# Latent attention: values and router logits made with weights as the stationary side over all 512 tokens, copied by ScalarE and turned by transposes

## The chip, the cores and the metric

The kernel runs on one core of one Trainium2 chip. The metric is the time of one launch on the device, in microseconds; less is better. The engines are TensorE (PE, matrix products and transposes into the PSUM banks), VectorE (DVE), ScalarE (ACT), GpSimd (POOL) and SyncE (SP), which issues most transfers.

## What is computed

Two layers over 8 sequences of 512 tokens with 256 features: softmax attention, a quantized feed-forward net, decaying linear attention, and last a step with latent attention and a sparse mixture of 8 experts. The change is in that last step's attention and router. Cut to it, the reference is:

```python
K = (hs @ k_w + k_b)   # 16 heads of 8
V = (hs @ v_w + v_b)   # 256 -> 128 features: 16 heads of 8
attn = softmax(Q[..., :8] @ K.T / sqrt(8), axis=-1)
ao = attn @ V                                   # 512 x 128, padded with zeros
mla_out = ao @ o_w + o_b                        # 512 x 256
probs = softmax(mla_out @ router_w + router_b)  # 512 x 8
topw, topi = top_k(probs, 2)
```

## The kernel before

Five parts run one after the other, each a block with its own program for every engine. The one of the change is `latent_attention` (from L1461). It handles one sequence per round and overlaps two: while the attention of one sequence is computed, the next one is loaded, turned and projected ("ahead"). A loop (`Fori`, in `turns`) runs 7 rounds; the ahead steps of the first sequence stand before it, and the rest of the last sequence behind it.

A round has 64 gaps (0 to 63), one for every unit of scores: 4 groups `a` of 4 heads, 4 blocks `t` of 128 keys, 4 heads `s`. The function `put(gap, engine, step)` places each step by hand, and every engine works through its steps strictly in the order of the gaps. Within a gap the pair S and ST comes first (A and TM ahead of it), and the steps that were put later stand behind. The steps, as "name(gap)" where the gap matters:

- S: scores of a unit, one product of 512 columns into one of 3 banks (`mla_ps_s`); M on VectorE takes their maximum. S of a bank waits for the M that empties it. S at gap 14 is the first unit of the next sequence; it needs the padded keys of that sequence and the M of gap 13.
- ST: the same scores, turned and shifted by the maximum, into one of 2 banks (`mla_ps_t`); X on ScalarE takes the exponential into `mla_pt`. ST waits for the X two units back.
- A: after every fourth unit, 4 products (8 instructions in the trace), probabilities times values (`mla_v`). OT copies the sum out.
- T, XH, XL: the next sequence's input is turned by TensorE and split into a high part (`xth`, ScalarE) and a low part (`xtl`, VectorE), so that three fp32r products give one product of full precision. `sum_of_parts` (L105 to L110) issues those three for each of the two blocks of 128 features; all its products carry line L110.
- Y(1) at gap 4, Y(0) at gap 6: queries and keys of the next sequence, weights stationary, 512 tokens moving: 6 products each for two column ranges. YH and YL split the results. Then SyncE copies them into `stack` (3 transfers for each side) and from there into `pad` (8 transfers, 4 for S and 4 for ST) for each group of heads.
- V at gap 10: the values. For each of 4 token blocks the tokens are the stationary side and the weights (128 columns) the moving one: 24 products of 128x128 into one bank `m`, so that the tokens lie on the partitions, as A needs them. VB on VectorE at gap 12 adds the bias (broadcast to all partitions) and copies to `vn`; VV on GpSimd copies into `mla_v` at gap 36.
- After the last A: BT, RI, AO, CT, CH, CL turn and split the attention's output; MT, MH and ML (gaps 50 to 53) make `mla_out` with the features on the partitions (`mth`, `mtl`).
- RL at gap 54: the router's logits, tokens stationary and the 8 columns of `router_w` moving, for 4 token blocks: 24 products of 128x8. LG on VectorE at gap 55 adds the bias, EX on ScalarE the exponential, and 21 small steps on VectorE up to gap 61 pick two experts. MO(0) and MO(1) at gaps 55 and 57 give `mla_out` with tokens on the partitions; POS at gap 62, PLACES and SC write the rows to the experts' lists.

All steps on TensorE but S, ST and A share two banks (`ps_m`) in turn; `emptied` names for each which engine's step frees its bank.

Of the kernel before, what the change touches and what calls it, by code (L numbers as in the profile page):

```python
# [21 lines left out]
ACT = mybir.ActivationFunctionType  # L22
# [3 lines left out]
P = 128  # L26
# [1434 lines left out]
def latent_attention(nc, const, x_in, sorted_out, counts, pieces_in, w, name):  # L1461
# [8 lines left out]
    with ctx:  # L1470
# [12 lines left out]
        vb, orow, rrow = sb("vb", [P, LAT]), sb("orow", [P, D]), sb("rrow", [P, E_])  # L1483
# [55 lines left out]
        def put(gap, eng, *keys, ahead=False):  # L1539
            if gap >= ROUND:  # L1540
                assert ahead
                gap, ahead = gap - ROUND, False
            gaps.setdefault((gap, eng), []).extend(keys)
            if ahead:
                ahead_keys[eng].update(keys)
# [18 lines left out]
        put(10, "tensor", ("V",), ahead=True); put(12, "vector", ("VB",), ahead=True)  # L1564
# [7 lines left out]
        put(end + 18, "tensor", ("RL",))  # L1572
# [13 lines left out]
        for eng in ("tensor", "vector", "scalar", "gpsimd"):  # L1586
# [6 lines left out]
        emptied = {"T": (dve_s, "XL"), "Y": (dve_s, "YL"), "V": (dve_s, "VB"), "BT": (dve_s, "AO"), "CT": (dve_s, "CL"),  # L1593
                   "POS": (dve_s, "PT"), "MT": (dve_s, "ML"), "MO": (dve_s, "MO"), "RL": (dve_s, "LG"), "TM": (dve_s, "QM")}
# [12 lines left out]
        with nc.Block() as block:  # L1607

            @block.sync
            def _(sp):  # L1610
                weights = [(raw_y[:, :, :], w["base"].rearrange("(k p) n -> p k n", p=P)), (raw_v[:, :, :], w["v_w"].rearrange("(k p) n -> p k n", p=P)),
                           (raw_r[:, :, :], w["router_w"].rearrange("(k p) n -> p k n", p=P)), (raw_o[:, 0, :], w["o_w"][0:P, :])]
                small = [(yb[:, :], w["base_b"]), (one_rows[:, :], w["one_rows"]), (vb[:, :], w["v_b"].partition_broadcast(P)),
# [47 lines left out]
            def _(pe):  # L1661
                own = owner("tensor")
                pe_s.start(pe)
                pe.wait_ge(zeroed, 3)

                def steps(i, run):
                    in_misc = [k for k in run if k in bank]
                    for key in run:
# [19 lines left out]
                        elif kind == "V":  # L1688
                            pe.wait_ge(weights_split, 2)
                            for t in range(TT):  # L1690
                                tok = slice(P * t, P * t + P)
                                last = sum_of_parts(nc, m[:, LAT * t:LAT * t + LAT], lambda k: xth[:, k, tok], lambda k: xtl[:, k, tok], lambda k: wvh[:, k, :], lambda k: wvl[:, k, :], KD)
# [47 lines left out]
                        elif kind == "RL":  # L1740
                            pe.wait_ge(*dve_s.at(j, "ML", KD - 1))
                            for t in range(TT):
                                tok = slice(P * t, P * t + P)
                                last = sum_of_parts(nc, m[:, E_ * t:E_ * t + E_], lambda k: mth[:, k, tok], lambda k: mtl[:, k, tok], lambda k: wrh[:, k, :], lambda k: wrl[:, k, :], KD)
# [13 lines left out]
            def _(dve):  # L1758
# [6 lines left out]
                dve.wait_ge(zeroed, 2)  # L1765
                nc.vector.memset(v[:, :, :, KPH:KPH + 1], 1.0).then_inc(zeroed, 1)
                dve.wait_ge(zeroed, 3)
# [45 lines left out]
                def steps(i, run):  # L1813
                    for key in run:
# [17 lines left out]
                        elif kind == "VB":  # L1832
                            dve.wait_ge(*pe_s.at(j, "V"))
# [644 lines left out]
```

## Time and profile before

| what | us |
|---|---|
| median of 3 runs | 3385.95 (3382.43 to 3387.80) |
| the profiled execution | 3384.29 |
| its span in the trace | 3382.5 |
| TensorE busy, of the span | 2859.8 (85%) |
| VectorE busy | 2033.0 (60%) |
| ScalarE busy | 1337.5 (40%) |
| latent attention in the trace | about 2210 to 3000 |

A row of the timeline has the start in us from the span's start, the length in us, engine, line, operation, output<-input, shape, count, and in brackets the idle time of the engine before it with what ended it. Matmuls overlap: the step from one start to the next is the price in a row of them, and the length is longer. PEld rows are loads of the stationary side.

### The profile page before, as it was taken

What the parts mean: (1) busy time and instruction counts of PE and PEld (TensorE: products, weight loads), DVE (VectorE), ACT (ScalarE), POOL (GpSimd) and SP (SyncE); (2) the same over time, 40 slices, a digit from 0 to 9 for tenths busy, and PEclk for the clock granted to TensorE, in tenths of its full rate; (3) what the DMA queues carried; (4) which work ended last, traced back from release to release, by engine and by line L of the source; (5) the groups of instructions that cost most, each with busy time, mean ns of one, the idle gap of its engine ahead of it and who ended that gap; (6) DMA issues with size and microseconds to landing.
All of it is one profiled execution on the core that took longest, in us unless ns stands there. A gap on an engine that the chain in (4) does not pass through costs nothing. (4 is left out here: it accounts for less than half of the span.)

```text
span 3382.5 us, 61649 instructions
## 1 busy us (share of the span) xinstructions
PE 2859.8 (85%) x16506; PEld 2062.8 (61%) x16507; DVE 2033.0 (60%) x3929; ACT 1337.5 (40%) x2815; POOL 965.4 (29%) x1303
## 2 busy tenths in 40 slices
PE   5998999989999958859999999868888888818992
PEld 4666666666666647747777777635544445417992
DVE  3666656566665568835666666566566566535664
ACT  3555554545545412222222222224444444424443
POOL 4334343343433211123333333210111111121225
PEclk8999999999999979979999999979888888868996
DMA  1101111011111021020000000031222211134225
GB/s 61 38 24 41 39 29 36 30 41 38 29 31 31 30 83 37 31 97 12 11 11 11 12 12 12 7 96 51 62 62 62 61 51 51 30 105 133 72 73 193
DMA packets 124632, 163.92 MB, mean 48 GB/s; under 512 B 19706, under 2 KB 87954, under 8 KB 123794
## 3 DMA queue, kind: packets, MB, share of 16 engines
q1 hardware_dynamic: 113300, 138.40, 13.9%
q0 software_dynamic: 6912, 18.96, 1.5%
q10 hardware_dynamic: 4224, 4.19, 0.4%
q8 instruction: 93, 1.52, 0.2%
q14 instruction: 103, 0.84, 0.1%
HBM read 87.73 MB, written 37.06 MB: 37 GB/s over the span
## 5 line engine op out<-in xcount | busy, mean ns | idle before, releaser
L1115 ACT ACTIVATE soft_probs<-soft_ps_s,soft_mx 128x512 f32<-128x512 f32 x512 | 347.9, 685 | 395.5 <-DVE soft_mx L1034 371.1
L1839 DVE TENSOR_REDUCE mla_mx<-mla_ps_s 128x1 f32<-128x512 f32 x512 | 334.2, 684 | 242.9 <-PE mla_ps_s L1699 225.3
L1034 DVE TENSOR_REDUCE soft_mx<-soft_ps_s 128x1 f32<-128x512 f32 x512 | 329.1, 684 | 236.9 <-PE soft_ps_s L944 224.3
L1942 ACT ACTIVATE mla_pt<-mla_ps_t 128x512 f32<-128x512 f32 x512 | 292.8, 600 | 397.5 <-PE mla_ps_t L1711 361.2
L944 PE MATMUL soft_ps_s<-soft_ks,soft_qs 128*128 128x512 f32 x1024 | 310.8, 423 | 10.3 <-ACT soft_probs L1115 10.3
L953 PE MATMUL soft_ps_p<-ident,soft_probs 128*128 128x128 f32 x2048 | 267.2, 273 | 12.6 <-issue 6.1
L953 PEld LDWEIGHTS soft_ps_p<-ident,soft_probs 128*128 128x128 f32 x2048 | 237.5, 141 | 47.5 <-issue 7.8
L944 PEld LDWEIGHTS soft_ps_s<-soft_ks,soft_qs 128*128 128x128 f32 x1024 | 171.6, 190 | 144.7 <-issue 59.2
L1044 DVE COPY soft_pt<-soft_ps_p 128x512 f32<-128x512 f32 x256 | 175.4, 685 | 137.3 <-PE soft_ps_p L953 134.6
L1699 PE MATMUL mla_ps_s<-mla_stack,mla_pad 128*128 128x512 f32 x512 | 236.0, 468 | 22.4 <-DVE mla_mx L1839 17.4
L962 PE MATMUL soft_ps_a<-soft_pt,soft_v 128*64 128x512 f32 x1024 | 251.9, 614 | 0.0
L1711 PE MATMUL mla_ps_t<-mla_shifted,mla_pad 128*128 128x512 f32 x512 | 226.2, 444 | 27.2 <-ACT mla_pt L1942 24.9
L407 PE MATMUL decay_ps_s<-decay_qs,decay_ks 128*128 128x512 f32 (+3 forms) x1024 | 192.1, 330 | 31.3 <-DVE decay_pt L523 30.5
L523 DVE TENSOR_TENSOR decay_pt<-decay_ps_s,decay_dec 128x512 f32<-128x512 f32 (+3 forms) x512 | 213.4, 480 | 4.7 <-PE decay_ps_s L407 4.7
L649 POOL TENSOR_TENSOR decay_rt<-decay_rt 128x256 f32<-128x256 f32 (+1 forms) x192 | 122.7, 661 | 300.7 <-DVE decay_rt L498 300.7
L407 PEld LDWEIGHTS decay_ps_s<-decay_qs,decay_ks 128*128 128x128 f32 x1024 | 169.2, 195 | 64.3 <-DVE decay_pt L523 44.0
L1699 PEld LDWEIGHTS mla_ps_s<-mla_stack,mla_pad 128*128 128x128 f32 x512 | 104.9, 205 | 165.9 <-DVE mla_mx L1839 74.7
L1122 ACT COPY soft_pt<-soft_ps_p 128x512 f32<-128x512 f32 x256 | 149.8, 585 | 81.5 <-PE soft_ps_p L953 70.5
L498 DVE TENSOR_TENSOR decay_rt<-decay_ps_m,decay_rope 128x1024 f32<-128x1024 f32 (+1 forms) x96 | 100.4, 1046 | 125.3 <-POOL decay_st L654 104.4
L313 ACT CAST decay_st<-decay_rt 128x512 fp32r<-128x512 f32 x64 | 39.6, 619 | 334.9 <-POOL decay_rt L649 197.4
L1711 PEld LDWEIGHTS mla_ps_t<-mla_shifted,mla_pad 128*128 128x128 f32 x512 | 103.0, 202 | 96.2 <-ACT mla_pt L1942 83.1
L1720 PE MATMUL mla_ps_a<-mla_pt,mla_v 128*32 128x512 f32 x1024 | 153.9, 676 | 6.5 <-ACT mla_pt L1942 4.8
(337 smaller groups left out, 6580.7 us busy)
## 6 DMA issues: line engine op xcount, KB each, us to landing
soft_rrep<-inverse SPq DMA_DIRECT2D x128, 128.0 KB, 2.9
mla_pad<-mla_stack SPq DMA_DIRECT2D x256, 64.0 KB, 2.0
moe_xt<-by_expert SPq DMA_DIRECT2D x72, 129.0 KB, 2.1
soft_ks<-soft_ks SPq DMA_DIRECT2D x64, 128.0 KB, 2.3
raw<-in_L_ffn_w SPq DMA_DIRECT2D x16, 512.0 KB, 8.6
mla_stack<-mla_yh SPq DMA_DIRECT2D x128, 64.0 KB, 2.1
soft_xc<-in_L_attn_x SPq DMA_DIRECT2D x8, 512.0 KB, 4.1
soft_xb<-in_L_attn_x SPq DMA_DIRECT2D x8, 512.0 KB, 4.1
```

The source lines that it names most:

```text
L407: last = nc.tensor.matmul(ps_s[:, t, P * t:SEQ], ks[:, n, g, P * t:P * t + P], qs[:, h, P * t:SEQ], start=(n == 0), stop=(n == 1))
L523: op = vv.tensor_tensor(weights_of(h, t), ps_s[:, t, P * t:SEQ], dec[:, h, 0:SEQ - P * t], ALU.mult)
L944: last = nc.tensor.matmul(ps_s[:, s_bank(n), :], qs[:, h, P * t:P * t + P], ks[:, b, g, :], start=(b == 0), stop=(b == 1))
L953: last = nc.tensor.transpose(ps_p[:, c % 2, P * t:P * t + P], probs[:, h % 2, t, P * c:P * c + P], ident[:, :])
L962: last = nc.tensor.matmul(ps_a[HD * s:HD * s + HD, 0, :], v[:, 1, c, HD * g:HD * g + HD], weights_of(2 * p + s, c), start=(c == 0), stop=( ...
L1034: op = vv.tensor_reduce(out=mx[:, h, t:t + 1], in_=ps_s[:, s_bank(4 * h + t), :], axis=AX.X, op=ALU.max, negate=True)
L1044: op = vv.tensor_copy(weights_of(h, c), ps_p[:, c % 2, :])
L1115: op = nc.scalar.activation(probs[:, h % 2, t, :], ps_s[:, s_bank(4 * h + t), :], ACT.Exp, bias=mx[:, h, t:t + 1], scale=1.0, accum_out=rs ...
L1699: last = nc.tensor.matmul(ps_s[:, (4 * t + s + 16 * a) % S_BANKS, :], pad[:, QUADS + a, s, P * t:P * t + P], stack[:, a, :], start=True, s ...
L1711: last = nc.tensor.matmul(ps_t[:, s % 2, :], pad[:, a, s, P * t:P * t + P], shifted[:, a, :], start=True, stop=True)
L1839: op = vv.tensor_reduce(out=mx[:, a, t, s:s + 1], in_=ps_s[:, (16 * a + 4 * t + s) % S_BANKS, :], axis=AX.X, op=ALU.max, negate=True)
L1942: op = nc.scalar.activation(pt[:, t % 2, s, :], ps_t[:, s % 2, :], ACT.Exp, scale=KPH ** -0.5)
```

## The change

V and RL are turned round. The weights become the stationary side and all 512 tokens move: 6 products of 512 columns instead of 24. The result then has the features (or the 8 experts) on the partitions. A copy on ScalarE takes it from PSUM to SBUF (VA to `vt`, with the bias now one value for each partition; RC to `lt`, 8 partitions of 128, of which the rest are set to zero once at the start), and 4 transposes on TensorE bring it back to tokens on the partitions (VT, RT). VB becomes a plain copy; LG adds the bias as before, from every 128th group of 8 columns.

The places move as well: V from gap 10 to 8, VA at 9, VT at 11, VB stays at 12; RL from 54 to 53, RC at 53, RT at 54, LG stays at 55. The two shared banks go on in turn with two more users.

The diff, cut to its core:

```diff
@@ -1480,7 +1480,8 @@
-        vb, orow, rrow = sb("vb", [P, LAT]), sb("orow", [P, D]), sb("rrow", [P, E_])
+        vb, orow, rrow = sb("vb", [P, 1]), sb("orow", [P, D]), sb("rrow", [P, E_])
+        vt, lt = sb("vt", [P, SEQ]), sb("lt", [P, SEQ])
@@ -1561,7 +1562,7 @@
-        put(10, "tensor", ("V",), ahead=True); put(12, "vector", ("VB",), ahead=True)
+        put(8, "tensor", ("V",), ahead=True); put(9, "scalar", ("VA",), ahead=True); put(11, "tensor", ("VT",), ahead=True); put(12, "vector", ("VB",), ahead=True)
@@ -1569,7 +1570,7 @@
-        put(end + 18, "tensor", ("RL",))
+        put(end + 17, "tensor", ("RL",)); put(end + 17, "scalar", ("RC",)); put(end + 18, "tensor", ("RT",))
@@ -1590,8 +1591,8 @@
-        emptied = {"T": (dve_s, "XL"), "Y": (dve_s, "YL"), "V": (dve_s, "VB"), "BT": (dve_s, "AO"), "CT": (dve_s, "CL"),
-                   "POS": (dve_s, "PT"), "MT": (dve_s, "ML"), "MO": (dve_s, "MO"), "RL": (dve_s, "LG"), "TM": (dve_s, "QM")}
+        emptied = {"T": (dve_s, "XL"), "Y": (dve_s, "YL"), "V": (act_s, "VA"), "VT": (dve_s, "VB"), "RT": (dve_s, "LG"), "BT": (dve_s, "AO"), "CT": (dve_s, "CL"),
+                   "POS": (dve_s, "PT"), "MT": (dve_s, "ML"), "MO": (dve_s, "MO"), "RL": (act_s, "RC"), "TM": (dve_s, "QM")}
@@ -1610,7 +1611,7 @@
-                small = [(yb[:, :], w["base_b"]), (one_rows[:, :], w["one_rows"]), (vb[:, :], w["v_b"].partition_broadcast(P)),
+                small = [(yb[:, :], w["base_b"]), (one_rows[:, :], w["one_rows"]), (vb[:, :], w["v_b"]),
@@ -1661,7 +1662,7 @@
-                pe.wait_ge(zeroed, 3)
+                pe.wait_ge(zeroed, 4)
@@ -1687,9 +1688,11 @@
+                            last = sum_of_parts(nc, m, lambda k: wvh[:, k, :], lambda k: wvl[:, k, :], lambda k: xth[:, k, :], lambda k: xtl[:, k, :], KD)
+                        elif kind == "VT":
+                            pe.wait_ge(*act_s.at(j, "VA"))
                             for t in range(TT):
-                                tok = slice(P * t, P * t + P)
-                                last = sum_of_parts(nc, m[:, LAT * t:LAT * t + LAT], lambda k: xth[:, k, tok], lambda k: xtl[:, k, tok], lambda k: wvh[:, k, :], lambda k: wvl[:, k, :], KD)
+                                last = nc.tensor.transpose(m[:, P * t:P * t + P], vt[:, P * t:P * t + P], ident[:, :])
@@ -1739,9 +1742,11 @@
+                            last = sum_of_parts(nc, m[0:E_, :], lambda k: wrh[:, k, :], lambda k: wrl[:, k, :], lambda k: mth[:, k, :], lambda k: mtl[:, k, :], KD)
+                        elif kind == "RT":
+                            pe.wait_ge(*act_s.at(j, "RC"))
                             for t in range(TT):
-                                tok = slice(P * t, P * t + P)
-                                last = sum_of_parts(nc, m[:, E_ * t:E_ * t + E_], lambda k: mth[:, k, tok], lambda k: mtl[:, k, tok], lambda k: wrh[:, k, :], lambda k: wrl[:, k, :], KD)
+                                last = nc.tensor.transpose(m[:, P * t:P * t + P], lt[:, P * t:P * t + P], ident[:, :])
@@ -1762,9 +1767,10 @@
-                dve.wait_ge(zeroed, 2)
+                nc.vector.memset(lt[:, :], 0.0).then_inc(zeroed, 1)
+                dve.wait_ge(zeroed, 3)
                 nc.vector.memset(v[:, :, :, KPH:KPH + 1], 1.0).then_inc(zeroed, 1)
-                dve.wait_ge(zeroed, 3)
+                dve.wait_ge(zeroed, 4)
@@ -1830,9 +1836,9 @@
-                            dve.wait_ge(*pe_s.at(j, "V"))
+                            dve.wait_ge(*pe_s.at(j, "VT"))
                             dve.wait_ge(*pool_s.at(shift(j, -1), "VV"))
-                            op = vv.tensor_tensor(vn[:, :, :], ps_m[:, bank["V",], :].rearrange("p (t n) -> p t n", n=LAT), vb[:, :].unsqueeze(1).broadcast_to([P, TT, LAT]), ALU.add)
+                            op = vv.tensor_copy(vn[:, :, :], ps_m[:, bank["VT",], :].rearrange("p (t n) -> p t n", n=LAT))
@@ -1873,8 +1879,8 @@
-                            dve.wait_ge(*pe_s.at(j, "RL"))
-                            op = vv.tensor_tensor(A3(lg), ps_m[:, bank["RL",], 0:TT * E_].rearrange("p (t e) -> p t e", e=E_), per_expert(rrow), ALU.add)
+                            dve.wait_ge(*pe_s.at(j, "RT"))
+                            op = vv.tensor_tensor(A3(lg), ps_m[:, bank["RT",], :].rearrange("p (t e) -> p t e", e=P)[:, :, 0:E_], per_expert(rrow), ALU.add)
@@ -1923,6 +1929,14 @@
+                        elif kind == "VA":
+                            act.wait_ge(*pe_s.at(j, "V"))
+                            act.wait_ge(*pe_s.at(shift(j, -1), "VT"))
+                            op = nc.scalar.activation(vt[:, :], ps_m[:, bank["V",], :], ACT.Identity, bias=vb[:, 0:1], scale=1.0)
+                        elif kind == "RC":
+                            act.wait_ge(*pe_s.at(j, "RL"))
+                            act.wait_ge(*pe_s.at(shift(j, -1), "RT"))
+                            op = nc.scalar.copy(lt[0:E_, :], ps_m[0:E_, bank["RL",], :])
@@ -2453,6 +2467,7 @@
+    host["L1_ffn_v_b"] = host["L1_ffn_v_b"].reshape(P, 1)
```

What stands on TensorE around V, in the loop. In the names, `mla_ps_s`, `mla_ps_t` and `mla_ps_a` are S, ST and A; L110 is a product of `sum_of_parts`. Before, from ST(8) to A(11), with the 24 products cut to the first three and the last:

```order
2007 L1711 MATMUL mla_ps_t<-mla_shifted,mla_pad 128x512
...
2009 L1699 MATMUL mla_ps_s<-mla_stack,mla_pad 128x512
...
2013 L1699 MATMUL mla_ps_s<-mla_stack,mla_pad 128x512
...
2015 L1711 MATMUL mla_ps_t<-mla_shifted,mla_pad 128x512
2016 L1675 REGISTER_ALU
2017 L110 MATMUL mla_ps_m<-mla_wvh,mla_xth 128x128
2018 L110 MATMUL mla_ps_m<-mla_wvl,mla_xth 128x128
2019 L110 MATMUL mla_ps_m<-mla_wvh,mla_xtl 128x128
...
2040 L110 MATMUL mla_ps_m<-mla_wvh,mla_xtl 128x128
2041 L1714 REGISTER_ALU
2042 L1720 MATMUL mla_ps_a<-mla_pt,mla_v 32x512 x4
```

And of the change, from ST(8) to VT at gap 11:

```order
1990 L1714 MATMUL mla_ps_t<-mla_shifted,mla_pad 128x512
1991 L1676 REGISTER_ALU
1992 L110 MATMUL mla_ps_m<-mla_xth,mla_wvh 128x512
1993 L110 MATMUL mla_ps_m<-mla_xtl,mla_wvh 128x512
...
1997 L110 MATMUL mla_ps_m<-mla_xth,mla_wvl 128x512
1998 L1701 REGISTER_ALU
1999 L1702 MATMUL mla_ps_s<-mla_stack,mla_pad 128x512
...
2007 L1723 MATMUL mla_ps_a<-mla_pt,mla_v 32x512 x4
...
2010 L1714 MATMUL mla_ps_t<-mla_shifted,mla_pad 128x512
...
2013 L1695 MATMUL mla_ps_m<-ident,mla_vt 128x128 x4
```

V now stands two units of scores earlier, ahead of S(9), and the transposes come after the A, S and ST of gap 11.

On TensorE around RL, before, from ST(53) over the 24 products (`mla_wrh`, `mla_wrl` are the router's weights) to A(55):

```order
2255 L1711 MATMUL mla_ps_t<-mla_shifted,mla_pad 128x512
2256 L1698 REGISTER_ALU
2257 L1699 MATMUL mla_ps_s<-mla_stack,mla_pad 128x512
2258 L1710 REGISTER_ALU
2259 L1711 MATMUL mla_ps_t<-mla_shifted,mla_pad 128x512
...
2262 L110 MATMUL mla_ps_m<-mla_wrh,mla_mth 128x8
...
2285 L110 MATMUL mla_ps_m<-mla_wrh,mla_mtl 128x8
...
2288 L1720 MATMUL mla_ps_a<-mla_pt,mla_v 32x512 x4
```

And of the change, from ST(53) to A(55):

```order
2222 L1714 MATMUL mla_ps_t<-mla_shifted,mla_pad 128x512
...
2225 L110 MATMUL mla_ps_m<-mla_mth,mla_wrh 8x512
...
2230 L110 MATMUL mla_ps_m<-mla_mth,mla_wrl 8x512
2231 L1701 REGISTER_ALU
2232 L1702 MATMUL mla_ps_s<-mla_stack,mla_pad 128x512
2233 L1713 REGISTER_ALU
2234 L1714 MATMUL mla_ps_t<-mla_shifted,mla_pad 128x512
2235 L1747 REGISTER_ALU
2236 L1749 MATMUL mla_ps_m<-ident,mla_lt 128x128 x4
...
2239 L1723 MATMUL mla_ps_a<-mla_pt,mla_v 32x512 x4
```

RL now stands ahead of S(54) and ST(54), and the transposes RT stand between them and A(55).

## Rows read from the trace of the kernel before

**Rows 1.** The page: busy time, share of the span and instructions of each engine.

```profile
PE 2859.8 (85%) x16506; PEld 2062.8 (61%) x16507; DVE 2033.0 (60%) x3929; ACT 1337.5 (40%) x2815; POOL 965.4 (29%) x1303
```

**Rows 2.** Timeline of TensorE in the second round, from S(9) to S(14).

```profile
2385.61 0.39 PE L1699 MATMUL mla_ps_s<-mla_stack,mla_pad 128*128 128x512 f32 x1
2388.50 0.80 PE L1711 MATMUL mla_ps_t<-mla_shifted,mla_pad 128*128 128x512 f32 x1 [2.50 <-ACT mla_pt L1942]
...
2390.16 0.31 PE L110 MATMUL mla_ps_m<-mla_wvh,mla_xth 128*128 128x128 f32 x1
...
2395.31 1.94 PE L1720 MATMUL mla_ps_a<-mla_pt,mla_v 128*32 128x512 f32 x8
...
2400.60 0.50 PE L1699 MATMUL mla_ps_s<-mla_stack,mla_pad 128*128 128x512 f32 x1 [1.03 <-DVE mla_mx L1839]
```

**Rows 3.** Stretches: length, busy times, then granted clock, DMA share, GB/s.

```profile
2388.00:2398.00 10.00, 9.50 (x37) 0.50 0.27 67
```

```profile
2290.00:2920.00 630.00, 551.65 (x2635) 313.87 (x2627) 391.82 (x823) 287.06 (x524) 65.97 (x104) 0.88 0.21 56
```

**Rows 4.** Timeline of ScalarE, then VectorE, same round: X(7), X(8) and X(9), YL(0).

```profile
2387.85 0.60 ACT L1942 ACTIVATE mla_pt<-mla_ps_t 128x512 f32<-128x512 f32 x1 [4.36 <-remote]
...
2388.91 1.09 ACT L1942 ACTIVATE mla_pt<-mla_ps_t 128x512 f32<-128x512 f32 x2
...
2389.06 0.75 DVE L1827 SCALAR_TENSOR_TENSOR mla_yl<-mla_ps_m,mla_yb,mla_yh 128x512 fp32r<-128x512 f32 x1
```

**Rows 5.** Timeline of TensorE in the first round: ST(53), RL's first product, A(55), S(55).

```profile
2347.43 0.39 PE L1711 MATMUL mla_ps_t<-mla_shifted,mla_pad 128*128 128x512 f32 x1
...
2349.83 0.27 PE L110 MATMUL mla_ps_m<-mla_wrh,mla_mth 128*128 128x8 f32 x1 [0.89 <-DVE mla_mtl L1831]
...
2354.48 1.94 PE L1720 MATMUL mla_ps_a<-mla_pt,mla_v 128*32 128x512 f32 x8
2356.34 0.80 PE L1699 MATMUL mla_ps_s<-mla_stack,mla_pad 128*128 128x512 f32 x1
```

**Rows 6.** Timeline of VectorE there: ML(1), M(55), LG.

```profile
2349.04 0.74 DVE L1831 SCALAR_TENSOR_TENSOR mla_mtl<-mla_ps_m,mla_ocol,mla_mth 128x512 fp32r<-128x512 f32 x1
...
2357.18 0.69 DVE L1839 TENSOR_REDUCE mla_mx<-mla_ps_s 128x1 f32<-128x512 f32 x1 [6.80 <-PE mla_ps_s L1699]
2357.79 0.18 DVE L1877 TENSOR_TENSOR mla_lg<-mla_ps_m,mla_rrow 128x32 f32<-128x32 f32 x1
```

**Rows 7.** Prices: products of Y, transposes, A and four gaps; a ScalarE copy (min/median/max ns).

```profile
2380.24 0.39 PE L110 MATMUL mla_ps_m<-mla_xth,mla_wyl 128*128 128x512 f32 x1
2380.47 0.40 PE L110 MATMUL mla_ps_m<-mla_xth,mla_wyh 128*128 128x512 f32 x1
...
2401.18 0.61 PE L1704 MATMUL mla_ps_m<-ident,mla_mrow 128*128 128x128 f32 x4
2401.72 1.07 PE L1720 MATMUL mla_ps_a<-mla_pt,mla_v 128*32 128x512 f32 x8
2402.72 0.50 PE L1699 MATMUL mla_ps_s<-mla_stack,mla_pad 128*128 128x512 f32 x1
...
2405.32 1.07 PE L1720 MATMUL mla_ps_a<-mla_pt,mla_v 128*32 128x512 f32 x8
```

```profile
L1947 ACT COPY mla_ot<-mla_ps_a x32: 578/580/590, 2274.1 to 2966.3; 128x512 f32<-128x512 f32 x32
```

**Rows 8.** Pad transfers of the second round; of the first sequence, with S that waits.

```profile
2392.16 5.12 SPq L1637 DMA_DIRECT2D mla_pad<-mla_stack  x8
```

```profile
2238.46 5.07 SPq L1637 DMA_DIRECT2D mla_pad<-mla_stack  x8
```

```profile
2242.41 10.21 PE L1699 MATMUL mla_ps_s<-mla_stack,mla_pad 128*128 128x512 f32 x17 [4.99 <-DMA mla_pad<-mla_stack]
```

**Rows 9.** Timeline of VectorE: memset at the start; LG of the last sequence.

```profile
2224.85 0.91 DVE L1764 MEMSET mla_mrow<- 128x1024 f32 x1 [0.16 <-issue]
...
2978.55 0.19 DVE L1877 TENSOR_TENSOR mla_lg<-mla_ps_m,mla_rrow 128x32 f32<-128x32 f32 x1 [3.00 <-PE mla_ps_m L110]
```

## The prediction

> **What bounds the kernel now.** First the page: TensorE is busy for 85% of the span and no other engine for more than 60% [rows 1]. That is a mean over stages, so the question is what the latent attention's own round looks like: 7 rounds of about 93 us, in each of which one sequence is attended to while the next one is prepared. I name places by the gap (0 to 63) in which the plan puts them. The timeline of TensorE round the step V (gap 10) and round RL (gap 54) is what the change bears on, so I read those two stretches, then the same microseconds on VectorE, ScalarE and SyncE's queue.
>
> At V [rows 2]: after the S of gap 9 TensorE idles 2.50 us for ScalarE; then ST(9), S(10), ST(10), and the 24 products of V, from 2390.16 to the next A at 2395.31, 5.15 us, 0.215 us each. The stretch 2388 to 2398 was granted 0.50 of the clock, which is the lower of the two levels, 1.2 GHz [rows 3]. S(14), the first product with the next sequence's scores, starts at 2400.60. The idle 2.50 us are not V's doing: ScalarE and VectorE both resume at 2387.8, ScalarE after 4.36 us put down to "remote" [rows 4]. Nothing in the code waits there for anything late, and its like stands in each of the 7 rounds. I take it as given.
>
> At RL [rows 5]: ML(1) on VectorE ends at 2349.78 [rows 6]; RL starts at 2349.83 and holds TensorE for 4.65 us until A(55); S(55) follows at 2356.34. Only when its maximum M(55) has run (2357.18) does VectorE come to LG (2357.79), after 6.80 us idle [rows 6]. From there the router's small operations keep VectorE nearly full to gap 62, so that what LG gains the whole tail of the round gains.
>
> So TensorE's in-order queue is the path at both places; V and RL sit on it with 24 short products each, whose price is that of 24 loads of stationary data.
>
> **The change, part by part.**
>
> V, removed: 5.15 us. Added at gap 8: 6 products of 512 columns at 0.23 us [rows 7] = 1.4 us at the full clock; at the lower one, by the ratio of an A (1.86 us against 1.00 us [rows 5, 7]), 2.6 us. V is now queued behind ST(8), in front of S(9): it falls into the 2.50 us in which TensorE waits for X(7) anyway, so its own cost is nothing; without that cover it would be 1.4 to 2.6. It is not waiting itself, since its bank was emptied by YL(1) and its operands by XL.
>
> VA on ScalarE: a 128x512 copy, 0.58 us [rows 7], with a bias some 0.1 more. It stands behind X(9), which ends at 2390.0 [rows 4], so it ends near 2390.7 and X(10) comes 0.6 later; ScalarE then waits for TensorE again, so this costs nothing. VT, four transposes, 0.54 us [rows 7] (0.7 to 0.8 at the lower clock), comes after ST(11) and finds VA done. VB stays one pass of 128x512 from PSUM on VectorE: no change.
>
> What is late next? Without V the same queue runs: ST(9), S(10), ST(10) from 2388.5, A(11) when X(9) is done at 2390.1, S and ST of 11, VT, then gaps 12 and 13, and M(12), VB, M(13) on VectorE: M(13) would be done at about 2394.6, or 2396.1 if the clock is low. But S(14) also needs the next sequence's padded keys. The chain is YL(0) (ends 2389.81 [rows 4]), three stack transfers, then four of the eight pad transfers, the first issued at 2392.16. In the first sequence, where TensorE waits for exactly this, the first pad transfer is issued at 2238.46 and S starts at 2242.41, 3.95 us on [rows 8]. So S(14) can start at 2396.1 and not before: the gain is 2400.60 - 2396.11 = 4.5 us, and the rest of V's 5.15 turns into a wait for the pad transfers.
>
> Of that some goes back. TensorE then idles some 1.3 us at gap 9, 0.6 at A(11), and up to 2.9 at S(14). In the trace the lower clock follows an idle of 2.50 us and lasts until about 2398. If it now falls at S(14), the steady stretch behind it, four gaps in 3.60 us at the full clock [rows 7], needs 1.86 us for the A and 8 x 0.43 (0.23 by the same ratio) for S and ST, 5.3 us, for the same four gaps: over 10 us that gives back 3.2 us. Bounds 1.3 to 4.5 us a round. I take 2.6 us: the fall in about 6 rounds of 10.
>
> RL. Removed 4.65 us, added 6 products of 8x512. No row shows 8 stationary columns; nearest are those of 128 columns and the same moving length, 0.23 us [rows 7], 1.4 us (2.6 at the lower clock). RL is moved up a gap, in front of S(54) and ST(54): TensorE waits for ML(1) from 2347.7 [rows 5] to the same 2349.8, and two products of 0.47 us that used to lie before RL now come behind it. RC on ScalarE waits for RL and takes 0.58 us, with X(54) queued behind it, which needs ST(54) anyhow; RT (0.54 to 0.7 us) waits for RC, with A(55) behind it. At the full clock: 2349.8, RL to 2351.2, S and ST run while RC runs to 2352.1, RT to 2352.6, A(55), S(55) at 2353.6, LG at 2355.0, 2.8 us earlier. At the lower clock throughout: RL to 2352.4, RC to 2353.3, RT to 2354.0, S(55) at 2355.9, LG at 2357.3, 0.5 us earlier. In the trace RL begins at full clock and loses it a few products later. I take 1.8 us.
>
> The Trainium skill (TensorE: Matmul & The Clock Gate, LDWEIGHTS) says a load takes its columns divided by 1.2, in ns, whatever the clock. By that V and RL would be 24 x 107 ns = 2.6 us each at either clock. The trace disagrees: 0.215 us a product at the lower clock. By the page the change would have some 2 us less to take from each, and both gains would be near their lower ends.
>
> Once only: the memset of lt (128x512) before TensorE's start, half of mrow's 0.91 us [rows 9], 0.45 us. In the first sequence V hides behind the pad chain already [rows 8], so V counts 7 times. In the last, RL runs alone at 0.11 us a product, LG comes 3.00 us after ML [rows 9]; 1.4 + 0.6 + 0.5 and the hand-overs between them are the same 3 us: nothing. So RL counts 7 times.
>
> Sum: 7 x (2.6 + 1.8) - 0.5 = 30 us. The profiled execution was 3384.29 us, 1.7 below the median of 3385.95; 30 less is 3354, and 3356 on the median. The ends: 7 x (1.3 + 0.5) - 0.5 = 12, 3374; 7 x (4.5 + 2.8) - 0.5 = 51, 3335.
>
> **The rivals.**
>
> 1. The stall at gap 7 depends on where instructions stand, and moves or goes. For: it ends at the same instant on two engines at the same gap in every round, and not in the last sequence, which doesn't prepare another. Against: up to it neither ScalarE's nor VectorE's instructions change. If it goes, YL(0) ends 2.6 us earlier and the pad chain with it, 18 us more in all: 3338. If a second one appears, 18 us less: 3374. The Trainium skill (Runtime: NRT & Kernel Launch, Instruction fetch mechanics) says that a taken branch out of the loaded pages stalls an engine until they are fetched; TensorE's program is 66 rows shorter now, so by it the stall could shift. No row says that this is the cause.
>
> 2. The gain is waited away: VT and RT stand in TensorE's in-order queue for a ScalarE copy. If ScalarE were late at both by the 2 us that are gained, the time is that of before, 3380 to 3386. For: every idle piece of TensorE in the steady stretch is a wait for ScalarE. Against: at both places ScalarE is idle before and after (4.36 us and more). The same time comes out if V and RL did not lie on the path, which the 6.80 us idle of VectorE speaks against.
>
> 3. Slower, by the clock. 44 short products a round, which kept TensorE without a gap, are replaced by 12 long ones and waits. At the lower clock four gaps take 5.3 instead of 3.6 us, 0.32 us lost per us spent there. A gain of 4.4 us a round is gone when the lower clock holds for 14 us more in each round than it does now; from there it is slower. With 20 us more: 7 x (0.32 x 20 - 4.4) = 14 us, 3400. Against: in the shown round V itself already runs at the lower clock.
>
> **How the numbers follow.** The forecast has 0.64, rival 1 0.14 (most of it still faster), rival 2 0.12, rival 3 0.07, anything else 0.03. A measurement here tells 0.2%, 7 us, from no change. The forecast's lower end of 12 us and rival 1 lie beyond that, rival 2 is within it for two thirds: faster 0.85, same 0.08, slower 0.07. The range 3335 to 3376 takes in the forecast's ends and both sides of rival 1 and leaves out rivals 2 and 3.
>
> **What would show it.** V's 6 products lie between 2.50 us of idle time's start and ST(9), and that idle is about 1.1 us. TensorE waits up to 2.9 us before S(14), which now names the pad transfers; S(14) comes 6.3 us after YL(0)'s end, not 10.8. RL takes 1.4 to 2.6 us; LG comes 5.2 to 7.5 us after ML(1), not 8.0. A round is 4.4 us shorter. I am wrong if S(14) stays 10 us behind YL(0), if the clock of the stage falls below its 0.88 [rows 3], or if RL's products of 8 columns run far from 0.23 us.

## Result and profile after

| | before | changed |
|---|---|---|
| median | 3385.75 us (4 runs) | 3359.67 us (4 runs) |
| range | 3382.43 to 3387.80 | 3355.20 to 3366.02 |
| profiled execution | 3384.29 | 3359.32 |
| its span | 3382.5 | 3357.5 |

The ratio is 0.9925, 95% interval 0.9907 to 0.9943: 26 us less, where 30 were forecast (3356, range 3335 to 3376). A second measurement of both gave 0.9937 (0.9925 to 0.9949).

The page's busy line of the changed kernel answers to [rows 1]; TensorE has 224 products and transposes fewer and is 46 us less busy. The row under it is the stretch of [rows 3], with the granted clock in the third column from the end, now 0.93 and not 0.88:

```profile
PE 2813.8 (84%) x16282; PEld 2012.2 (60%) x16283; DVE 2033.4 (61%) x3930; ACT 1343.6 (40%) x2831; POOL 964.2 (29%) x1303
...
2290.00:2920.00 630.00, 525.90 (x2522) 273.31 (x2522) 410.20 (x866) 304.05 (x557) 76.11 (x120) 0.93 0.21 58
```

TensorE in the second round, from V to the S behind S(14); it answers to [rows 2]. V's six products start right behind ST(8), 0.23 us each, and the idle time at ST(9) is 1.27 us instead of 2.50. S(14) now waits, and it names the pad transfers:

```profile
2384.85 0.39 PE L110 MATMUL mla_ps_m<-mla_xth,mla_wvh 128*128 128x512 f32 x1
...
2386.00 0.40 PE L110 MATMUL mla_ps_m<-mla_xth,mla_wvl 128*128 128x512 f32 x1
2386.23 0.39 PE L1702 MATMUL mla_ps_s<-mla_stack,mla_pad 128*128 128x512 f32 x1
2387.89 0.50 PE L1714 MATMUL mla_ps_t<-mla_shifted,mla_pad 128*128 128x512 f32 x1 [1.27 <-ACT mla_pt L1956]
...
2392.16 1.05 PE L1695 MATMUL mla_ps_m<-ident,mla_vt 128*128 128x128 f32 x4
...
2395.63 0.49 PE L1702 MATMUL mla_ps_s<-mla_stack,mla_pad 128*128 128x512 f32 x1 [1.49 <-DMA mla_pad<-mla_stack]
...
2396.72 1.06 PE L1723 MATMUL mla_ps_a<-mla_pt,mla_v 128*32 128x512 f32 x8
2397.71 0.50 PE L1702 MATMUL mla_ps_s<-mla_stack,mla_pad 128*128 128x512 f32 x1
```

VectorE, YL(0) of that round [rows 4]; it ends at 2389.20, so S(14) comes 6.43 us later:

```profile
2388.45 0.75 DVE L1833 SCALAR_TENSOR_TENSOR mla_yl<-mla_ps_m,mla_yb,mla_yh 128x512 fp32r<-128x512 f32 x1
```

TensorE at S(14) of the third round: 3.12 us of waiting, and the A behind it takes 1.58 us to the next S instead of 0.99, since the lower clock (1.2 GHz) has come:

```profile
2483.81 0.49 PE L1702 MATMUL mla_ps_s<-mla_stack,mla_pad 128*128 128x512 f32 x1 [3.12 <-DMA mla_pad<-mla_stack]
...
2484.90 1.65 PE L1723 MATMUL mla_ps_a<-mla_pt,mla_v 128*32 128x512 f32 x8
2486.48 0.79 PE L1702 MATMUL mla_ps_s<-mla_stack,mla_pad 128*128 128x512 f32 x1
2487.07 0.63 PE L1714 MATMUL mla_ps_t<-mla_shifted,mla_pad 128*128 128x512 f32 x1
```

Three of the things that TensorE waited for between 2280 and 2900 us: us in total, times, the longest. The pad transfers, which before stood only ahead of the first sequence [rows 8], are there in each of the seven rounds:

```profile
PE mla_ps_s L1702 <- DMA mla_pad<-mla_stack: 19.2, 7, 3.1
PE mla_ps_s L1702 <- DVE mla_mx L1845: 16.5, 14, 1.9
PE mla_ps_m L110 <- DVE mla_mtl L1837: 14.0, 7, 2.0
```

RL in the first round on TensorE (against [rows 5]) and in the third, then ML(1) and LG of the first on VectorE (against [rows 6]). Six products of 8 columns have the price of those of 128, 0.23 us. In the third round the clock falls within them and they take 2.0 us instead of 1.4:

```profile
2352.45 0.40 PE L110 MATMUL mla_ps_m<-mla_mth,mla_wrh 128*8 128x512 f32 x1 [2.00 <-DVE mla_mtl L1837]
...
2354.75 0.66 PE L1749 MATMUL mla_ps_m<-ident,mla_lt 128*128 128x128 f32 x4 [0.27 <-ACT mla_lt L1939]
2355.34 1.06 PE L1723 MATMUL mla_ps_a<-mla_pt,mla_v 128*32 128x512 f32 x8
2356.34 0.50 PE L1702 MATMUL mla_ps_s<-mla_stack,mla_pad 128*128 128x512 f32 x1
...
2528.95 0.40 PE L110 MATMUL mla_ps_m<-mla_mth,mla_wrh 128*8 128x512 f32 x1 [2.00 <-DVE mla_mtl L1837]
...
2529.68 0.63 PE L110 MATMUL mla_ps_m<-mla_mth,mla_wrh 128*8 128x512 f32 x1
2530.10 0.63 PE L110 MATMUL mla_ps_m<-mla_mtl,mla_wrh 128*8 128x512 f32 x1
...
2531.89 1.12 PE L1749 MATMUL mla_ps_m<-ident,mla_lt 128*128 128x128 f32 x4
```

```profile
2351.66 0.74 DVE L1837 SCALAR_TENSOR_TENSOR mla_mtl<-mla_ps_m,mla_ocol,mla_mth 128x512 fp32r<-128x512 f32 x1
...
2357.49 0.18 DVE L1883 TENSOR_TENSOR mla_lg<-mla_ps_m,mla_rrow 128x32 f32<-128x32 f32 x1
```

To see where the time went I cut every round at five marks: the starts of YL(1), YL(0), S(14), ML(1) and LG. Means in us over the seven rounds of the loop (LG to the next YL(1): six):

| piece | before | changed | before, again | changed, again |
|---|---|---|---|---|
| YL(1) to YL(0) | 4.86 | 4.74 | 4.71 | 4.73 |
| YL(0) to S(14) | 10.79 | 7.17 | 10.97 | 7.16 |
| S(14) to ML(1) | 43.32 | 44.31 | 43.08 | 44.31 |
| ML(1) to LG | 7.37 | 6.31 | 6.89 | 6.31 |
| LG to YL(1) | 26.05 | 25.95 | 26.28 | 25.96 |

In the first pair V gives 3.62 us up to S(14) and loses 0.99 behind it, 2.63 net; RL gives 1.06. Seven rounds: 18.4 + 7.4 = 25.8. The small rest: 1.5 us in the other two pieces, 1.0 lost in the last sequence (63.05 us between its LG and the one before, then 64.04). From the first YL(0) to the last LG the changed kernel is 26.3 us shorter; that YL(0) came 1.6 us later, and the span is 25.0 us shorter.

### The profile page after: what moved, and what is told of

Its sections match the earlier page's. It is cut to its first block and busy times, and to the rows that moved or that the text cites. A ratio compares the mean times of both kernels' runs of the same rounds, so it can differ in the third digit from the quotient of the medians.

```text
span 3357.5 us, 61264 instructions
## 1 busy us (share of the span) xinstructions
PE 2813.8 (84%) x16282; PEld 2012.2 (60%) x16283; DVE 2033.4 (61%) x3930; ACT 1343.6 (40%) x2831; POOL 964.2 (29%) x1303
## 5 line engine op out<-in xcount | busy, mean ns | idle before, releaser
L1714 PE MATMUL mla_ps_t<-mla_shifted,mla_pad 128*128 128x512 f32 x512 | 218.5, 429 | 17.6 <-ACT mla_pt L1956 15.1
L1143 POOL TENSOR_TENSOR soft_rt<-soft_rt 128x256 f32<-128x256 f32 (+1 forms) x192 | 120.2, 647 | 133.9 <-DVE soft_rt L1021 133.9
```

What stands on the lines that cost most here:

```text
L1714: last = nc.tensor.matmul(ps_t[:, s % 2, :], pad[:, a, s, P * t:P * t + P], shifted[:, a, :], start=True, stop=True)
```

## The experiments

The question is not whether the time fell but why: by the form (six long products for 24 short ones) or by the place; whether the two parts add up; whether the lower clock behind S(14) comes from the wait; and what the stall at gap 7 is, on which the cover of V rests. The twelve runs fell on three chips. On the first (e1 to e4) and the third (e12) the kernel before takes 3341 and 3342 us, on the second (e5 to e11) 3384, as in the result above. All ratios are to the kernel before on the same chip.

**e1, e2 and e4: parts alone, with a flaw of mine.** With one part undone TensorE has 21 steps on the two shared banks, an odd number, so that the last one of a round, TM(2), falls on the bank of T(0). I set POS to the other bank and overlooked TM(2):

```diff
         bank = {k: n % 2 for n, k in enumerate(misc)}
+        bank["POS",] = 1
```

> V as in the change, RL as before. Theory: in the traces of before and after, the way from YL(0) to the first S of the next sequence (gap 14) is 3.6 us shorter in the mean of the 7 rounds, and the lower clock behind that S takes back 1.0, so V is worth 2.6 us a round: 18 us, 3367. S(14) comes 7.2 us after YL(0)'s start in every round and names the pad transfers. Rival (the two parts need each other, by the two shared banks or by the clock that one leaves to the other): 3374 or more, and S(14) later than 7.2 us in some rounds.

> RL as in the change, V as before. Theory: ML(1) to LG is 1.06 us shorter in the mean of 7 rounds, LG to the next YL(0) 0.2, less 0.5 once: 8 us, 3378. Rival (RL is worth what the first round alone showed, 2.8 us): 20 us, 3366.

> V in the new form with VA and VT, but at the old place (V at gap 10, VA 11, VT 12, VB 13), RL as before. Theory of the place: V costs 1.4 to 2.6 us on the path and VT 0.6 to 0.8, instead of 5.15, so S(14) is 1.8 to 3.2 us earlier than before: 12 to 22 us, 3364 to 3374, likeliest 3371, a little behind V alone. Rival (the form makes all the gain): 3367 as V alone. Rival (ScalarE's copy at gap 11 is waited for): 3380.

Measured, against 3341.41 us for before: V alone 3360.68 us, ratio 1.0052 (1.0038 to 1.0066); RL alone 3356.51, 1.0037 (1.0023 to 1.0051); the new V at gap 10 3360.71, 1.0048 (1.0034 to 1.0061). All three are slower than before, and the trace of e1 says where, in the second round at T(0) on TensorE:

```profile
2380.19 1.11 PE L1683 MATMUL mla_ps_m<-ident,mla_xc 128*128 128x128 f32 x4 [2.41 <-DVE mla_shifted L1858]
```

T(0) waits for QM(2) (`mla_shifted`), the reader of TM(2)'s bank. LG to YL(1) is 27.3 us here and 27.4 and 27.7 in the two others; in e3, with its even number of steps, 25.1. So none of the three says what its part is worth. Two things stand all the same. In e1 and e4 S(14) comes 7.16 us after YL(0) in both, and the times agree: with V at gap 8 or at gap 10, the new form costs the same on this chip. (Other pieces differ and even out: S(14) to ML(1) is 43.71 us in e1 and 43.05 in e4.) And in all of them YL(1) to YL(0) is 3.5 us in every round: the stall at gap 7 isn't there. In e2, which has V as before, the 24 products then run at 0.11 us each, and S(14) comes 7.63 us after YL(0), not 10.8; the first round of before, the only one without a stall, has the same 7.63.

**e3 and e10: the place without the form.** One edit to the kernel before:

```diff
-        put(10, "tensor", ("V",), ahead=True); put(12, "vector", ("VB",), ahead=True)
+        put(8, "tensor", ("V",), ahead=True); put(12, "vector", ("VB",), ahead=True)
```

> The kernel before with V's 24 products of 128x128 moved from gap 10 to gap 8, nothing else. Theory (the place makes V's gain, not the form): the 24 products run at the full clock there, 0.11 us each, 2.6 us, in the 2.5 us in which TensorE waits for X(7); S(14) then waits for the pad transfers as in the change: 3367, as V alone. Rival (the form makes it): at 0.215 us a product V takes 5.15 us wherever it stands, ST(9) is 2.6 us late, S(14) hardly earlier than before: 3380 to 3386.

> The kernel of e3 again: before, with V's 24 products moved from gap 10 to gap 8. Theory (the place makes V's gain, the form hardly any): where the stall stands at gap 7, the 24 products fall into the idle time behind ST(8) at the full clock, 2.6 us in all, S(14) comes 7.2 us after YL(0) as in the changed kernel, and the ratio is that of V alone, 0.9966 (0.995 to 0.998). Rival (the form makes it): V takes 5.15 us there, S(14) comes 9 us or more after YL(0), and the ratio is 0.999 to 1.001.

Measured on the first chip 3340.79 us, 0.9990 (0.9981 to 0.9999); on the second 3371.11, 0.9962 (0.9950 to 0.9975). TensorE in e10, third round, V's first products, its last one, S(9), ST(9) and S(14):

```profile
2471.89 0.22 PE L110 MATMUL mla_ps_m<-mla_wvh,mla_xth 128*128 128x128 f32 x1
...
2472.06 0.27 PE L110 MATMUL mla_ps_m<-mla_wvh,mla_xtl 128*128 128x128 f32 x1
...
2474.45 0.27 PE L110 MATMUL mla_ps_m<-mla_wvh,mla_xtl 128*128 128x128 f32 x1
2474.56 0.44 PE L1699 MATMUL mla_ps_s<-mla_stack,mla_pad 128*128 128x512 f32 x1
...
2475.58 0.50 PE L1711 MATMUL mla_ps_t<-mla_shifted,mla_pad 128*128 128x512 f32 x1
...
2482.28 0.79 PE L1699 MATMUL mla_ps_s<-mla_stack,mla_pad 128*128 128x512 f32 x1 [3.29 <-DMA mla_pad<-mla_stack]
```

The 24 products take 2.67 us, the ST(9) behind them has no idle time ahead of it, and S(14) waits for the pad transfers as in the changed kernel. That is the theory's side, within 0.02 us (7.19 against 7.17 after YL(0)). So the place alone is enough for V's gain where the stall stands. What the form alone would give there was not measured: the new form at the old place (e4) ran only on the first chip. There, without the stall, the edit of e3 gives 0.1%: by the pieces 7.63 less 7.19 us a round, 3 us in all; by the medians 0.6 us.

**e7 and e8: both kernels again.** Unchanged, since before took 44 us less on the first chip than in the result.

> The kernel before, unchanged, for its trace where it takes 3341 us and not 3386. Theory (the stall at gap 7 is the difference): YL(1) to YL(0) is 3.5 us in each of the 7 rounds and not 4.6 to 6.0, TensorE keeps the full clock behind it, V's 24 products take 2.6 us and not 5.15, S(14) comes 7.6 us after YL(0) and not 11.2: 6 rounds x (1.4 + 3.7) = 31 of the 44 us lie there. Rival: the latent attention is as before and the 44 us lie in other stages.

> The changed kernel, unchanged, beside before on the same chip. Theory (V's gain is that of the stall and its lower clock): without the stall V gives only 0.4 us a round (S(14) 7.2 instead of 7.6 us after YL(0)) and RL 0.5 to 1.1, so 6 to 10 us: a ratio of 0.997 to 0.998. Rival (the gain of 26 us does not hang on the stall): 0.992. Rival (with V in front of S(9) and no idle time there, ST(9) is late by 1.4 us a round, and two more waits): 1.003.

These two fell on the second chip, and there before takes 3383.02 us again (1.0000, 0.9989 to 1.0010) and the changed kernel 3361.48 (0.9937, 0.9925 to 0.9949), with the stall in rounds 2 to 7 of both. So what either takes without the stall was not seen in a trace of its own; e3, which differs from before in V's place only, is the nearest: 85.9 us a round instead of 92.2. In the last sequence the changed kernel loses 4.3 us here (67.53 against 63.25), 1.0 in the first pair.

**e5 and e6: parts alone, with both banks set.**

```diff
         bank = {k: n % 2 for n, k in enumerate(misc)}
+        bank["POS",], bank["TM", 2] = 0, 1
```

> V alone again, with the shared banks set by hand so that T(0) no longer takes the bank of TM(2), whose QM it waited for by 2.4 us a round in e1. Theory: LG to the next YL(1) falls from 27.3 to 25.2 us, 14 us; V itself gives 0.4 us a round against before on the same chip: 0.999, and 0.9945 if before has the stall there. Rival (the extra wait at the loop's start has another cause, such as the code's length): 1.005 again.

> RL alone again with the same correction. Theory: as V alone, LG to YL(1) falls by 2 us; ML(1) to LG 6.6 instead of 7.1 to 7.4 us, 3 to 6 us in all: 0.998 to 0.999. Rival (RL keeps the 1.06 us a round of the first pair of traces, and LG to YL(1) another 0.2): 0.9975.

V alone 3372.40 us, 0.9966 (0.9953 to 0.9979); RL alone 3380.71, 0.9988 (0.9979 to 0.9997). LG to YL(1) is 26.25 and 25.94 us: the extra wait is gone. Both keep the theory's signs, but V alone misses the 0.9945 expected where the stall is, and the parts don't add up: 11.7 + 3.4 us of the medians against 22.6 for both. By pieces:

| piece, mean us | before, again | V alone | RL alone | both |
|---|---|---|---|---|
| YL(0) to S(14) | 10.97 | 7.17 | 10.81 | 7.16 |
| S(14) to ML(1) | 43.08 | 43.96 | 43.08 | 44.31 |
| ML(1) to LG | 6.89 | 7.66 | 6.31 | 6.31 |
| last sequence, LG to LG | 63.25 | 70.30 | 67.49 | 67.53 |

Each part does at its own place what it does in the changed kernel. But with V alone the old RL costs more than before: 8.55, 8.69 and 8.82 us in rounds 2 to 4, 6.4 to 7.9 in before. Its 24 products meet the lower clock more often, at 0.21 us each instead of 0.11; the new RL loses at most 1.2 us to it (5.8 us at the full clock, 7.0 at the lower one). The other part of the gap lies in the last sequence. What brings the clock down there more often was not tried apart. The gap is known roughly only: the pieces of V alone are those of its slowest execution (3378.48 us, 6 above its median), so a part of the 8.7 us a round and of the 70.30 may be that execution's own.

**e11: does the wait bring the clock down?** Ten products that nobody reads, after ST(13):

```diff
+        put(13, "tensor", ("FL",), ahead=True)
...
+                        elif kind == "FL":
+                            for n in range(10):
+                                last = nc.tensor.matmul(m, wvh[:, 0, :], xth[:, 0, :], start=True, stop=True)
```

> The changed kernel with ten products of 128x512 more on TensorE after ST(13), 2.3 us at the full clock, into a shared bank that nobody reads: they fill the 3.1 us in which TensorE waits for the pad transfers. Theory (the lower clock behind S(14) comes from that idle time and costs 1.3 us): S(14) to ML(1) falls from 44.3 to 43.1 us in 6 of 7 rounds, S(14) itself stays 7.2 us after YL(0) but for 0.8 in the second round: 7 to 9 us faster than the changed kernel with 70 products more, 0.991 to 0.992 of before. Rival (the lower clock has another cause): S(14) to ML(1) stays at 44.3 us and the time at 0.9937 or a little above.

Measured 3353.71 us, 0.9912 (0.9896 to 0.9929), 8 us less than the changed kernel by the medians. S(14) to ML(1) is 43.03 us in the mean and never over 43.05; S(14) stays 7.16 us after YL(0). TensorE in the third round, the ten products, S(14), and the A and S behind it (against 2484.90 and 2486.48 above):

```profile
2474.88 2.49 PE L1696 MATMUL mla_ps_m<-mla_xth,mla_wvh 128*128 128x512 f32 x10
2478.14 0.49 PE L1707 MATMUL mla_ps_s<-mla_stack,mla_pad 128*128 128x512 f32 x1 [0.76 <-DMA mla_pad<-mla_stack]
...
2479.23 1.06 PE L1728 MATMUL mla_ps_a<-mla_pt,mla_v 128*32 128x512 f32 x8
2480.22 0.50 PE L1707 MATMUL mla_ps_s<-mla_stack,mla_pad 128*128 128x512 f32 x1
```

So the lower clock behind S(14) was the price of the idle time ahead of it, 1.3 us a round. Work that fills a wait and is thrown away makes the kernel faster. Of the 9 us that this gives in seven rounds 2.4 are lost again at RL: there the clock now falls in five rounds and not in three, and ML(1) to LG is 6.65 us instead of 6.31.

The idle time is needed for the fall, but its length alone doesn't decide. With V alone (e5) TensorE waits as long ahead of S(14) in rounds 5 to 7, and the clock stays up: the A behind it takes 1.00 us to the next S, and S(14) to ML(1) is 43.0 us. The fifth round of e5:

```profile
2674.60 0.49 PE L1703 MATMUL mla_ps_s<-mla_stack,mla_pad 128*128 128x512 f32 x1 [3.11 <-DMA mla_pad<-mla_stack]
...
2675.68 1.06 PE L1724 MATMUL mla_ps_a<-mla_pt,mla_v 128*32 128x512 f32 x8
2676.68 0.50 PE L1703 MATMUL mla_ps_s<-mla_stack,mla_pad 128*128 128x512 f32 x1
```

In e1 the same holds for 2.36 us in rounds 1 to 4, while behind 2.36 us in the first round of the changed kernel the clock fell. What else it takes isn't shown.

**e9: what is the stall at gap 7?** In the changed kernel's third round, ScalarE resumes at 2475.40, 2.06 us after GpSimd has issued the last of its eight indirect transfers (SC); the first round has none before it and no stall. GpSimd, then ScalarE:

```profile
2472.38 0.96 POOL L2019 DMA_INDIRECT by_expert<-mla_mo,mla_place_i  x1 [0.30 <-issue]
```

```profile
2475.40 0.60 ACT L1956 ACTIVATE mla_pt<-mla_ps_t 128x512 f32<-128x512 f32 x1 [3.06 <-PE mla_ps_s L1702]
```

The edit holds the transfers back until the maximum of gap 9 of the next round:

```diff
+                                if not isinstance(i[0], int):
+                                    hold(pool, *dve_s.at(shift(j, 1), "M", 3, 2, 3))
                             op = nc.gpsimd.indirect_dma_start(...)
```

> The changed kernel, but GpSimd holds its eight indirect transfers (SC) of a sequence until the maximum at gap 9 of the next round has run (not for the last sequence). Theory (the stall at gap 7 is bound to these transfers: it ends 1.6 to 2.1 us after the last of them is issued, and the first round, with none before it, has no stall): YL(1) to YL(0) is 3.5 us in all 7 rounds instead of 4.7 to 6.1; the stall is gone, and 8 to 20 us with it (0.988 to 0.991 of before), or it comes back 10 gaps later and the time stays at 0.9937. Rival (the stall is bound to the place in the program, by instructions that arrive late after the loop's jump): it stays at gap 7 with 4.7 and 6.1 us, wherever the transfers are.

Measured 3373.99 us, 0.9968 (0.9956 to 0.9980): slower than the changed kernel. YL(1) to YL(0) is 3.48 us in all seven rounds, so the stall has left gap 7. It is back behind S(14), 16 us later. GpSimd's last transfer in the third round, the S(15) that TensorE has long done, and VectorE's and ScalarE's first step behind the stall:

```profile
2488.74 0.96 POOL L2021 DMA_INDIRECT by_expert<-mla_mo,mla_place_i  x1 [0.30 <-issue]
```

```profile
2488.32 0.50 PE L1702 MATMUL mla_ps_s<-mla_stack,mla_pad 128*128 128x512 f32 x1
```

```profile
2491.98 0.69 DVE L1845 TENSOR_REDUCE mla_mx<-mla_ps_s 128x1 f32<-128x512 f32 x1 [5.75 <-remote]
```

```profile
2492.01 1.78 ACT L1956 ACTIVATE mla_pt<-mla_ps_t 128x512 f32<-128x512 f32 x3 [5.35 <-remote]
```

In the changed kernel M starts 0.5 us after its S; M(15) starts at 2491.98, 3.1 us later than that, and 2.3 us after the last issue. No instruction of TensorE, VectorE or ScalarE stands elsewhere than in the changed kernel. The stall follows the transfers and not the place in the program. At its new place it costs more: S(14) to ML(1) is 47.33 us against 44.31, since there TensorE, in the steady stretch, stands idle ahead of an ST, for 2.7 to 3.0 us in five of the six rounds with the stall. The lower clock has little part in that: it fell at S(14) as in the changed kernel, and a second time behind the stall only in the last two rounds (48.5 us each). Why the last transfer holds up the others' waits, and why it doesn't on two of the chips, stays open. The Trainium skill (DMA: Bandwidth & Descriptors, Anatomy of one DMA — SWDGE (gpsimd) path) gives a transfer on this path a fixed cost of some 2.0 us, most of it until the last byte is confirmed as landed. The 1.6 to 2.3 us here agree with a stall that ends when the last transfer has landed; in the traces with the stall, the last packet of the queue that carries them ended 0.1 to 1.0 us before VectorE went on. That other engines should wait for it no sentence there says.

**e12: two more edits on top of e11.** Five filling products ahead of RL, and RT a gap later:

```diff
-        put(end + 17, "tensor", ("RL",)); put(end + 17, "scalar", ("RC",)); put(end + 18, "tensor", ("RT",))
+        put(end + 17, "tensor", ("FR",), ("RL",)); put(end + 17, "scalar", ("RC",)); put(end + 19, "tensor", ("RT",))
```

> The kernel of e11 with two edits more: five filling products after ST(53), ahead of RL, in the 2.0 us in which TensorE waits for ML(1); and the transposes RT moved from gap 54 to 55, behind A(55), S(55) and ST(55), so that M(55), which stands ahead of LG on VectorE, no longer waits for RC and RT. Theory (RL's way is 1.15 us longer in the rounds in which the lower clock falls behind that wait, and RT lies on the way to S(55) with 0.9 us): ML(1) to LG falls from 5.8 or 7.0 us to 4.9 in every round, 10 to 12 us, 0.9876 to 0.988 of before. Rival (the fill is too short to keep the clock, its first product waits for ML(0)): ML(1) to LG is 4.9 or 6.0, 0.989. Rival (LG then waits for RT instead): 5.8 and 7.0 as now, 0.991.

It fell on the third chip: 3325.96 us against 3342.22, 0.9951 (0.9937 to 0.9964), so the expected ratios can't be read against it. What can is ML(1) to LG: 5.24 to 5.28 us in each of the seven rounds, mean 5.26, where e11 has 5.8 or 7.0. The clock is kept (no record of the lower one at RL in any round); the last third of a microsecond is the filling itself, which ends after ML(1) and starts RL late. TensorE in the second round: the fill, RL, A(55), S(55), RT:

```profile
2436.73 1.44 PE L1696 MATMUL mla_ps_m<-mla_xth,mla_wvh 128*128 128x512 f32 x5 [0.75 <-DVE mla_mtl L1842]
2438.30 0.39 PE L110 MATMUL mla_ps_m<-mla_mth,mla_wrh 128*8 128x512 f32 x1
...
2440.26 1.07 PE L1728 MATMUL mla_ps_a<-mla_pt,mla_v 128*32 128x512 f32 x8
2441.25 0.50 PE L1707 MATMUL mla_ps_s<-mla_stack,mla_pad 128*128 128x512 f32 x1
...
2441.82 0.60 PE L1754 MATMUL mla_ps_m<-ident,mla_lt 128*128 128x128 f32 x4
```

Against e3 on a chip where before takes the same time (3341.41 and 3342.22) it is 15 us faster. The changed kernel was not measured on such a chip, nor e12 on one with the stall; that e12 beats e11 there is an inference from the pieces (9.7 us in seven rounds). Which of the two edits gave how much was not tried apart.

## Why the prediction was right, and where it was not

**The bound at V.** Right. The queue of TensorE was the path, V left it, and the pad transfers took its place: 6.3 us after YL(0)'s end were forecast, 6.43 measured in the second round; in the mean YL(0) to S(14) is 7.17 us in seven rounds that differ by 0.2. The gain is 4.15 us in rounds 2 to 7, near the 4.5 worked out. In the first it is 0.44, since [rows 2] are of the second round, and there is no stall in the first: that the term counts six times and not seven was missed; the prediction read the stall into "each of the 7 rounds".

**The clock at S(14).** The mechanism was right (e11), its size twice off: the lower clock falls in 6 of 7 rounds, not in 6 of 10, and costs 1.3 to 1.5 us each time, not 3.2, because it holds for 3.4 us there, by the clock's record in the trace, and not for 10. The product, 1.0 us a round instead of 1.9, made good for the missed first round: that the term of 2.6 us came out at 2.63 is luck, two errors that cancel.

**Where V's gain comes from.** The prediction said that V's own cost would be hidden in the idle time, and so it is. What it left unsaid is that the form isn't needed for it. The old 24 products at gap 8 give the same (e10), because at the full clock they take 2.67 us and at gap 10, behind the stall, 5.15. The stall taken "as given" was both the cover and the reason for the price: where it is absent, V's place is worth 3 us or less in all (e3).

**RL.** The mis-sized term: 1.8 us a round forecast, 1.06 measured (0.58 in the second pair). [rows 5, 6] are of the first round, where ML(1) to LG took 8.75 us, the longest of all; the mean of before is 7.37. The new form does what was worked out: 1.4 us at the full clock, 2.0 where the clock falls within it, and LG 5.1 to 6.3 us after ML(1)'s end, at the lower end of the 5.2 to 7.5 forecast. The base was wrong, not the change.

**The price of a short product.** The Trainium skill (TensorE: Matmul & The Clock Gate, LDWEIGHTS) gives a load as its columns divided by 1.2, in ns, 107 for 128 columns, and unlike the formulas for products above it names no clock for it. The prediction took that as either clock. The 24 products of e10 agree with it at the full clock, 0.11 us each; those of [rows 2] at the lower one took 0.215. So it was right to follow the trace; by the page V would have looked half as dear.

**The rivals.** The first (the stall hangs on the place of instructions) fell as a mechanism: 66 rows fewer on TensorE left it at gap 7, and moving the transfers moved it. Its other half came true once, in the changed kernel's last sequence, where before has no stall: ScalarE waits until 1.6 us after the last transfer's issue at 2917.53. That is part of the 1.0 us lost there, and of the 4.3 in the second pair.

```profile
2919.09 2.28 ACT L1956 ACTIVATE mla_pt<-mla_ps_t 128x512 f32<-128x512 f32 x4 [2.33 <-PE mla_ps_s L1702]
```

The second (ScalarE's copies are waited for) shows in one place: RT starts 0.27 to 0.29 us late for RC in four of seven rounds; VT doesn't wait in the loop. The third (slower by the clock) fell: 0.93 instead of 0.88. Its mechanism is real all the same: 7 us of the 25 that V gained up to S(14) went back through it. (The short products that it counted as 44 a round are 48; no term hangs on that.)

**The rest.** The memset and the last sequence were sized at 0.5 us and nothing; the first YL(0) came 1.6 us later, of which 1.1 lay before the stage began. A round was to be 4.4 us shorter and is 3.7 (92.44 and 88.75), 3.4 in the second pair.

## What to carry to other kernels

Ask for every step on the path at which clock it runs and why: a step that stands behind a stall can cost twice what it costs two gaps earlier, and moving it may give all that a new form gives. Take the base of a term from the mean of all rounds, and ask which round has the stall and which has not. Where a wait can't be removed, work that is thrown away may be cheaper than the idle time (here it was, by 8 us). And with shared banks taken in turn, count the steps: an odd number ties the last one of a round to the first of the next.

## What the runs showed of the hardware

- After the eight indirect transfers of GpSimd, VectorE and ScalarE stood still for some 3 us although what they wait for was done, until 1.6 to 2.3 us after the last issue; this moved with the transfers (e9). It was in all seven kernels that ran where before takes 3384 us, and in none of the five that ran where it takes 3341 or 3342.
- At S(14) the granted clock fell behind an idle time of 3.1 us on TensorE in the changed kernel and did not behind one of 0.76 us (e11); behind 1.49 us in the second round of the changed kernel it did not either. But it also stayed up behind 3.1 us in three rounds of e5 and behind 2.36 us in four of e1. Where it fell in the changed kernel at S(14) it held for 3.4 us.
- A product of 512 columns with 8 stationary columns cost 0.23 us at the full and 0.43 us at the lower clock, the same as with 128.
